# First cross-attention of a decoder: two pairs of score banks, sums turned token-major, three buffers of keys and values

## What is computed

```python
q = x @ Wq.T + bq
k = context @ Wk.T + bk
v = context @ Wv.T + bv
q = q.reshape(B, NQ, 16, 16); k = k.reshape(B, NKV, 16, 16); v = v.reshape(B, NKV, 16, 16)
attn = jnp.einsum('bihd,bjhd->bhij', q, k) * SCALE
attn = jax.nn.softmax(attn, axis=-1)
out = jnp.einsum('bhij,bjhd->bihd', attn, v).reshape(B, NQ, 256)
x = _layernorm(x + out @ Wo.T + bo)
```

## Time and profile before

| | |
|---|---|
| median of 3 runs | 2735.5 us (2731.75 to 2739.67) |
| profiled execution | 2742.5 us, its span 2740.6 us |
| mean granted TensorE clock | 0.86 |
| busy, share of the span | PE 79%, weight loads 55%, DVE 59%, ACT 27%, POOL 33% |
| chain that ended last | PE 58%, DVE 23%, POOL 7%, DMA 4%, ACT 4% |
| of it, `enc_w<-v_all_scratch` DMA | 3% |
| scores L884, PE, x512 | 144.8 us busy; idle before it 120.3 us |
| row maxima L1039, DVE, x128 | 120.3 us busy, 940 ns each |
| shifted scores L897, PE, x1536 | 134.9 us busy |
| exp L1007, ACT, x128 | 93.5 us busy, 730 ns each |
| DMA | 101.22 MB, mean 37 GB/s |

### The profile page before, as it was taken

How to read it: one execution, slowest core, us unless ns; L and a number is a source line. 1 busy time by engine, 2 the same in 40 slices (tenths; PEclk the granted TensorE clock), 3 DMA queues, 4 the chain that set the end, 5 groups by cost and what they waited for, 6 DMA issues and landing times.

```text
span 2740.6 us, 36682 instructions
## 1 busy us (share of the span) xinstructions
PE 2173.6 (79%) x14852; PEld 1517.0 (55%) x14852; DVE 1608.5 (59%) x3034; ACT 734.0 (27%) x1387; POOL 894.8 (33%) x715
## 2 busy tenths in 40 slices
PE   7787777577669997899999999987666786767776
PEld 2333345455546665787888888776454553434532
DVE  7888835355542332455555565566399996455245
ACT  6545232223221122222222222222222221111122
POOL 7886349916300002343534434332200002110000
PEclk9888878788778998899999999998767657888987
DMA  4212233111110001000100100100331010400000
GB/s 135 80 47 85 76 61 105 35 52 46 41 38 30 1 1 73 1 1 1 60 1 1 60 1 1 45 1 1 90 68 34 26 30 24 95 0 0 1 0 27
DMA packets 63592, 101.22 MB, mean 37 GB/s; under 512 B 32361, under 2 KB 56930, under 8 KB 62210
## 3 DMA queue, kind: packets, MB, share of 16 engines
q1 hardware_dynamic: 63426, 98.90, 12.5%
HBM read 78.39 MB, written 20.50 MB: 36 GB/s over the span
## 4 chain that ended last, share of the span: by engine, by line
PE 58%; DVE 23%; POOL 7%; DMA 4%; ACT 4%; issue 3%; SPq 0%; POOLq 0%; DVEq 0%; ACTq 0%
PE PS L1422 8%; PE PS L1438 7%; PE PS L1178 4%; DVE st_h L682 4%; DVE top L2176 3%; PE PS L1157 3%; DVE w_s L2185 3%; PE PS L1339 3%; DMA enc_w<-v_all_scratch 3%; PE PS L884 2%; PE PS L2062 2%; DVE ln_st L265 2%; PE PS L2052 2%; PE PS L1367 2%; DVE XD L1039 2%
## 5 line engine op out<-in xcount | busy, mean ns | idle before, releaser
L284 POOL TENSOR_SCALAR ln_ve<-ln_mv 128x2 f32<-128x2 f32 (+1 forms) x91 | 20.2, 222 | 1491.4 <-DVE ln_mv L268 1491.2
L884 PE MATMUL PS<-enc_w,q_s 32*112 32x375 f32 x512 | 144.8, 604 | 120.3 <-DVE XD L1039 64.3
L1614 DVE TENSOR_TENSOR p_x<-PS,cols 128x1024 f32<-128x1024 f32 x112 | 129.3, 1217 | 147.6 <-PE PS L1384 147.6
L1676 POOL TENSOR_TENSOR q_x<-q_f,cols 128x2048 f32<-128x2048 f32 x56 | 208.7, 3746 | 9.7 <-ACT q_f L1534 9.7
L1039 DVE TENSOR_REDUCE XD<-PS 112x2 f32<-112x750 f32 x128 | 120.3, 940 | 140.0 <-PE PS L884 140.0
L682 DVE TENSOR_TENSOR_SCAN st_h<-dA,st_h 128x3584 f32<-128x3584 f32 x16 | 183.8, 11512 | 0.0
L1007 ACT ACTIVATE e_t<-PS 125x672 f32<-125x672 f32 x128 | 93.5, 730 | 287.0 <-PE PS L897 287.0
L774 POOL TENSOR_TENSOR st_h<-b_s,XD 128x896 f32<-128x896 f32 x56 | 166.3, 3005 | 8.1 <-PE PS L492 6.8
L884 PEld LDWEIGHTS PS<-enc_w,q_s 32*112 32x112 f32 x512 | 51.9, 200 | 162.7 <-DVE XD L1039 97.3
L1242 DVE SCALAR_TENSOR_TENSOR XA<-PS,gate_w,XA 112x256 f32<-112x256 f32 x128 | 61.9, 484 | 135.4 <-PE PS L1178 135.4
L1946 PE MATMUL PS<-dg,e_p 112*125 112x112 f32 x384 | 83.9, 415 | 66.1 <-ACT dg L2130 66.1
(11 more groups left out here) (351 smaller groups left out, 4905.5 us busy)
## 6 DMA issues: line engine op xcount, KB each, us to landing
v_all_scratch<-v_st SPq DMA_DIRECT2D x16, 750.0 KB
enc_w<-v_all_scratch SPq DMA_DIRECT2D x16, 750.0 KB
t_ring<-k_scratch SPq DMA_DIRECT2D x8, 784.0 KB, 12.2
enc_w<-in_enc_w SPq DMA_DIRECT2D x2, 3072.0 KB, 10.6
wc<-in_enc_w SPq DMA_DIRECT2D x2, 3072.0 KB, 10.7
k_all_scratch<-k_st SPq DMA_DIRECT2D x16, 375.0 KB
enc_w<-k_all_scratch SPq DMA_DIRECT2D x64, 93.8 KB
ctx_k<-in_ctx SPq DMA_DIRECT2D x16, 281.2 KB
```

The source lines that it names most:

```text
L884: ins = pe.matmul(ps[a][0:T, 0:S2], q_s[h, m, b * T:(b + 1) * T], k_s[h, b % 2, m, :], start=True, stop=True)
L1614: last = dve.tensor_tensor(p_x[:, m, :, :, :], ps[1][:, m * P:(m + 1) * P].rearrange("p (h i) -> p h i", i=16).unsqueeze(2) .to_broadcast( ...
L1676: last = pool.tensor_tensor(q_x[:, c, :, :].rearrange("p t (h i) -> p t h i", i=16), q_f[:, k % 2, c, :].rearrange("p (t i) -> p t i", i=1 ...
```

## The change

1. Scores have two pairs of banks (0, 1 and 2, 3, by the parity of the pair), and AHEAD is 6; a pair's scores wait for the maximum of the pair before the last. Shifted scores have banks 4 and 5, the weighing bank 6, and all other uses share bank 7, each waiting for the one before it. `nm_w` has four buffers. `slot_uses` gives each use a slot of its own, and a pair of maxima is turned one slot earlier.
2. The sums of a batch are turned to have tokens on partitions (`turn_sums`, 4 matmuls of 112 x 4), inverted there (112 x 16) and spread by 16 matmuls of 32 x 112; DVE multiplies out of PSUM.
3. Keys and values have three buffers; keys and values each have semaphores of their own; values are awaited by `weigh`. Three batches of keys, then the output weights, then three of values and the experts' weights are loaded ahead. `v_t` has moved out of `enc_w0`, `wo4` into it.
4. POOL makes no unit ahead of the first root, then 5, 5 and 4.
5. Each transposed half of the residual has its own signal (`xt_ready`), so later stages count on from `TURNED_X`.

```diff
@@ xat_load @@
-            for b in range(B):
-                if b >= 2:
-                    sp.wait_ge(st_ready, 8 * (b - 1))
...
+            for b in range(3):
+                load_keys(b)
+            sp.dma_start(wo4[:, :, :], dr["wo4"]).then_inc(wo_loaded, 16)
+            sp.wait_ge(y_copied, len(UNITS))
+            for b in range(3):
+                load_values(b)
+            moe_load(sp)
+            for b in range(3, B):
+                sp.wait_ge(st_ready, 8 * (b - 2))
+                load_keys(b)
+                sp.wait_ge(av_done, 4 * (b - 2))
+                load_values(b)
@@ slot_uses @@
-            if at % 2 and 0 <= n + 1 < PAIRS:
-                uses.append(("max", (n + 1) // 2))
...
+            if at % 2 and 0 <= n + 3 < PAIRS:
+                uses.append(("max", (n + 3) // 2))
+            if at == 0 and 0 <= b < B - QB:
+                uses.append(("q", 4 * (b // QB + 1) + b % QB))
...
+            if at == 2 and 1 <= b <= B:
+                uses.append(("rs", b - 1))
+            if at == 4 and 1 <= b <= B:
                 uses.append(("sum", b - 1))
+            if at == 6 and 1 <= b <= B:
                 uses.append(("wo", b - 1))
+            if at in (2, 4) and b > QB and b % QB == 2:
+                uses.append(("xt", 2 * (b // QB) - 2 + (at == 4)))
@@ xat_claim @@
-            if n >= 3:
-                before, j = XAT_USES[n - 3]
+            if n >= 4:
+                before, j = XAT_USES[n - 1]
@@ xat_pe: score @@
-                    if n >= 1:
-                        pe.wait_ge(max_done, n)
+                    if n >= 2:
+                        pe.wait_ge(max_done, n - 1)
                 h = slice(32 * r, 32 * r + 32)
-                ins = pe.matmul(ps[a][0:T, 0:S2], q_s[h, m, b * T:(b + 1) * T], k_s[h, b % 2, m, :],
+                ins = pe.matmul(ps[2 * (n % 2) + a][0:T, 0:S2], q_s[h, m, b * T:(b + 1) * T], k_s[h, b % 3, m, :],
@@ xat_pe: weigh @@
+                if m == 0:
+                    pe.wait_ge(v_loaded[b % 3], V_0[b % 3] + 16 * (b // 3 + 1))
@@ xat_pe @@
+            def turn_sums(b):
+                bank = xat_claim(pe, "rs", b)
+                pe.wait_ge(ot_copied, b + 1)
+                for m in range(4):
+                    last = pe.matmul(bank[0:T, 4 * m:4 * m + 4], o_t[:, m * T:(m + 1) * T], ident[:, 16:P:32],
+                                     start=True, stop=True)
+                last.then_inc(rs_ready, 1)
+
             def spread_sums(b):
                 bank = xat_claim(pe, "sum", b)
-                pe.wait_ge(ot_copied, b + 1)
-                for r in range(4):
-                    last = pe.matmul(bank[32 * r:32 * r + 32, 0:4 * T],
-                                     ident[:, 32 * r + 16:32 * r + 17].to_broadcast([P, 32]), o_t[:, :],
-                                     start=True, stop=True)
+                pe.wait_ge(rs_done, RS_0 + b + 1)
+                for m in range(4):
+                    for r in range(4):
+                        last = pe.matmul(bank[32 * r:32 * r + 32, m * T:(m + 1) * T],
+                                         rs_s[:, 4 * m + r:4 * m + r + 1].to_broadcast([T, 32]),
+                                         ident[0:T, 0:T], start=True, stop=True)
@@ xat_dve @@
-                        link(dve.reciprocal(o_n[:, :], xat_bank("sum", i)[:, 0:4 * T]))
-                        dve.tensor_tensor(o_n[:, :], o_t[:, :], o_n[:, :], ALU.mult).then_inc(divided, 1)
+                        dve.tensor_tensor(o_n[:, :], o_t[:, :], xat_bank("sum", i)[:, 0:4 * T], ALU.mult)\
+                            .then_inc(divided, 1)
@@ xat_pool @@
-                for unit in range(4 * q, min(4 * q + 4, KC * KHIGH)):
+                for unit in range((0, 0, 5, 10)[q], (0, 5, 10, KC * KHIGH)[q]):
```

More of the change, by code:

```diff
@@ L786, in build @@
             sem("kg_arg"), sem("kg_trig"), sem("kg_done"), sem("k_stored"))
-        PAIRS, AHEAD = B * 8, 5
-        kv_loaded, KV_0 = [z_ready, z_abs], len(UNITS)
+        PAIRS, AHEAD = B * 8, 6
+        k_loaded, K_0 = [z_ready, z_abs, bc_ready], (len(UNITS), len(UNITS), NQ)
+        v_loaded, V_0 = [bc_copied, bc_split, u_done], (NQ, NQ, len(UNITS))
+        rs_ready, rs_done, RS_0 = dA_ready, scan_done, 2 * len(UNITS)
         q_ready, q_copied = sem("q_ready"), sem("q_copied")
@@ L841, in build @@
         XAT_AT = {u: i for i, u in enumerate(XAT_USES)}
-        XAT_FREED = {"q": (q_copied, 0), "max": (max_added, 0),
+        XAT_FREED = {"q": (q_copied, 0), "max": (max_added, 0), "rs": (rs_done, RS_0),
                      "sum": (divided, 0), "wo": (wo_added, 0), "xt": (xf_ready, 8), "x1": (xf_ready, 6)}
         def xat_bank(kind, i):
-            return ps[5 + XAT_AT[(kind, i)] % 3]
+            return ps[4 + i] if kind == "q" and i < 4 else ps[7]
         def xat_claim(pe, kind, i):
@@ L909, in weigh @@
                 pe.wait_ge(exp_done, 2 * g + 2)
-                if m == 0 and b >= 1:
-                    pe.wait_ge(ot_copied, b)
+                if m == 0:
+                    pe.wait_ge(v_loaded[b % 3], V_0[b % 3] + 16 * (b // 3 + 1))
+                    if b >= 1:
+                        pe.wait_ge(ot_copied, b)
                 for j in range(JC):
@@ L914, in weigh @@
                         h = 4 * m + r
-                        last = pe.matmul(ps[4][32 * r:32 * r + 32, m * T:(m + 1) * T],
-                                         v_t[0:JR, b % 2, j, 32 * h:32 * h + 32],
+                        last = pe.matmul(ps[6][32 * r:32 * r + 32, m * T:(m + 1) * T],
+                                         v_t[0:JR, b % 3, j, 32 * h:32 * h + 32],
                                          e_t[0:JR, (2 * g + r // 2) % 4, r % 2, j * T:(j + 1) * T],
@@ L943, in turn_input @@
                                         XA[0:T, B - QB + k, i * P:(i + 1) * P], ident[0:T, 0:T])
-                if i == KC - 1:
-                    last.then_inc(xt_ready, 1)
+                last.then_inc(xt_ready, 1)
             def turn_residual(i):
@@ L953, in turn_residual @@
                                         XA[0:T, q * QB + k, c * P:(c + 1) * P], ident[0:T, 0:T])
-                if c == KC - 1:
-                    last.then_inc(xt_ready, 1)
-            shared = {"q": queries, "max": turn_max, "sum": spread_sums, "wo": project,
+                last.then_inc(xt_ready, 1)
+            shared = {"q": queries, "max": turn_max, "sum": spread_sums, "rs": turn_sums, "wo": project,
                       "xt": turn_residual, "x1": turn_input}
@@ L962, in xat_pe @@
                 ahead, uses = n + AHEAD, slot_uses(n)
-                if uses and uses[0][0] == "max":
-                    turn_max(uses[0][1])
                 if 0 <= ahead < PAIRS:
@@ L981, in xat_pe @@
                 for kind, i in uses:
-                    if kind in ("sum", "wo", "xt"):
+                    if kind not in ("q", "x1"):
                         shared[kind](i)
@@ L1006, in xat_act @@
                         act.wait_ge(av_done, n // 2 - 1)
-                    act.activation(e_t[0:JR, n % 4, :, :], PS[0:JR, 2:4, 0:JC * T], ACT.Exp).then_inc(exp_done, 1)
+                    act.activation(e_t[0:JR, n % 4, :, :], PS[0:JR, 4:6, 0:JC * T], ACT.Exp).then_inc(exp_done, 1)
                 for kind, i in uses:
@@ L1049, in xat_dve @@
                 ahead, uses = n + AHEAD, slot_uses(n)
-                if uses and uses[0][0] == "max":
-                    add_max(uses[0][1])
                 if 0 <= ahead < PAIRS:
@@ L1054, in xat_dve @@
                 for kind, i in uses:
-                    if kind == "sum":
+                    if kind == "max":
+                        add_max(i)
+                    elif kind == "rs":
+                        dve.wait_ge(rs_ready, RS_0 + i + 1)
+                        dve.reciprocal(rs_s[:, :], xat_bank("rs", i)[0:T, 0:16]).then_inc(rs_done, 1)
+                    elif kind == "sum":
                         dve.wait_ge(sum_ready, i + 1)
```

73 lines of the change are left out of this document (32 added, 41 removed).

## The result

| | before | changed |
|---|---|---|
| median | 2736.07 us (4 runs, 2731.75 to 2739.67) | 2857.78 us (4 runs, 2853.08 to 2865.01) |
| ratio | 1 | 1.0446, interval 1.0429 to 1.0464 |
| profiled execution, its span | 2742.5, 2740.6 us | 2862.3, 2860.5 us |
| first exp to last exp | 411.7 us | 540.7 us |

The change makes the kernel 4.5% slower. I had forecast 2720 us, in a range of 2655 to 2762: wrong in sign and outside the range.

The account below looks back on a forecast made before the run. Bounds: the score-maximum ring, DMA waits with low clock behind, POOL's stall. Stage 342 + 57 = 399 us against 411.7, with the tail called -15, gave a 2720 us median; own range 2700 to 2745, 8 in 10 2655 to 2762.

Parts of the forecast that it names:

- The ring of 2.02 us: In the kernel before, scores, row maximum and back to PE with one score pair, setting each slot's length.
- Part (a): Stage's slots: two score pairs cut the maximum's wait, even AHEAD queues passes in strips; slot 2.69 us, 342 in all.
- exp ring: Shifted scores, exp and back to shifted scores: 1.82 us, the next limit once two score pairs are used.
- Part (b): Stage's other PE work (projection, spreading, turned sums, queries, residual transposes, norm stalls), paid beyond some 0.4 us free: 57 us.
- rival 2: Stage slower: clock still falls once a batch, 16 stretches costing 42 to 51 us, giving say 2766 us; chance 0.13.
- my own case: The forecast's main case for the whole kernel: granted clock 1.00 through the stage, 2700 to 2745 us, chance 0.58.
- Part (c): Key and value loads: three buffers remove the 51.6 us of waits and each batch's low clock; added early loads cost nothing.
- Part (d): Sums of each batch: 2.96 us of DVE reciprocal go, a 112x16 one comes; DVE is no bound.
- Part (e): First norm: with no POOL unit ahead of the first root, the 16 us stall goes; later groups fit between norms.
- Part (f): Stage's ends: no gain at the start, bounds 0 and 5 us; the tail changes by -1.5 us.
- Rival 1: Strips do not hold each other up: slot 1.82 + 0.06, 103 us less, 2617 us; chance 0.13 (half-way form 2668, 0.10).
- Rival 3: Matmuls on PE start in program order, so second-head scores wait: 32 us slower, 2752 us; chance 0.06.

## Why the prediction was wrong

**Right: what bounds the kernel before, and the mechanism of the strips.** The ring of 2.02 us, the DMA waits, and that with an even AHEAD the passes of a slot queue in their strips. The last was shown from both sides (AHEAD 5 and 7 in the changed kernel, 4 in the kernel before).

**Part (a), the slot: right in kind, too large.** 2.69 us was forecast, 2.44 is measured at the full clock. I had added 2 x 0.40 and 0.06 to the exp ring. In the rows above the second head's score passes start 0.41 us apart and the shifted pass 0.31 behind the second, 0.72 together; and the 0.1 us by which a second strip starts late is not added to them but falls inside, for the score pass starts with the first head's shifted pass. 0.62 is paid and not 0.87. I had also given every slot this length. In a slot with a weighting the exp is done before PE comes to the shifted scores, and PE's own list sets the time. At the full clock:

```profile
588.35 1.77 PE L879 MATMUL PS<-XF,wb 128*128 128x448 f32 x4
590.05 0.78 PE L929 MATMUL PS<-e_t,v_t 125*32 125x112 f32 x24
590.77 0.89 PE L896 MATMUL PS<-enc_w,q_s 32*112 32x375 f32 x4
591.49 0.81 PE L909 MATMUL PS<-q_s,enc_w 32*125 32x112 f32 x12
592.23 0.32 PE L917 MATMUL PS<-ident,XD 112*128 112x112 f32 x1
...
595.38 0.95 PE L939 MATMUL PS<-ident,XD 128*112 128x4 f32 x8
```

Weighting, scores and shifted scores are 2.18 us (590.05 to 592.23).

**Part (b): too small.** I had let 0.4 us of each addition go free. In the slots with a weighting almost nothing is free: the queries are paid with 1.70 (588.35 to 590.05; forecast 1.1). The kernel with both heads' scores first has the same order in these slots, so its exps give the others, as what a slot has above 2.18:

```profile
585.40 0.73 ACT L1024 ACTIVATE e_t<-PS 125x672 f32<-125x672 f32 x1 [1.09 <-PE PS L909]
588.35 0.73 ACT L1024 ACTIVATE e_t<-PS 125x672 f32<-125x672 f32 x1 [2.22 <-PE PS L909]
590.17 0.73 ACT L1024 ACTIVATE e_t<-PS 125x672 f32<-125x672 f32 x1 [1.09 <-PE PS L909]
594.26 0.73 ACT L1024 ACTIVATE e_t<-PS 125x672 f32<-125x672 f32 x1 [3.36 <-PE PS L909]
```

Spreading is paid with 0.77 (585.40 to 588.35; forecast 0.3), the projection with 1.91 (590.17 to 594.26; forecast 1.55). The turned sums, 8 passes in 0.95 (L939 above), are paid with some 0.9 (forecast 0.4).

**The sum of the stage: near at the full clock, by luck.** 60 plain slots of 2.44, 3 of 1.82 at the end and 64 slots of 2.18 are 291 us, where I had 342. Queries (20), turned sums, spreading and projection of 15 batches (53) and some 21 for the three norms and the residual transposes are 94 us, where I had 57. Together that is some 385 us, an estimate from the rows above and the same slots of the scores-first kernel. The forecast of 399 is near it because one term was some 50 us too large and the other some 40 too small.

**The step that failed: rival 2, its price and with it its chance.** By that estimate the lower clock costs some 155 us (540.7 - 385). I had let the clock fall once a batch, for the 6.8 us or so for which it falls behind a DMA wait before, and priced 16 such stretches at 42 to 51 us with a chance of 0.13; my own case had the clock at 1.00 throughout. In fact the clock does not wait for idle time: it is at 0.52 from 422 to 442 us with PE busy in all 20.00, and low for 72% of the stage. My argument against was the end of the stage, a stretch of some 6 us in which shifted scores and weighting alone run at the short times. So short a stretch, with side-by-side slots in front of it, says nothing of 540 us. The trace even has the clock fall right behind it: the next weighting takes 1.35 us in place of 0.78, after 0.82 us of idle time.

```profile
798.07 1.35 PE L915 MATMUL PS<-e_t,enc_w 125*32 125x112 f32 x24 [0.82 <-ACT e_t L1007]
```

The row that did bear on it I had in hand and named: leading pairs of scores on two strips, at the low clock, 1.59 in place of 0.89. It does not settle the matter, since PE is idle 1.04 us ahead of such a pair. But I used it for 6.8 us a batch, when the changed kernel puts two strips at a time into every slot of the stage. The price for a microsecond fits. By it (2.6 to 3.2 us in each 6.8) the 389 us at the lower level cost 149 to 183 us, and 2720 becomes 2869 to 2903. The number of stretches was wrong: these are the length of 57 and not of 16, and the sign was to turn at five.

**Also in rival 2, the link to the layout.** How busy PE is does not tell the kernels apart: it is busy for 98% of the stage with the change (clock 0.64), 96% with AHEAD 5 (0.87), and 81% where scores wait for the maximum again (0.93). The same matmuls, in the same number, had 0.64 one behind the other and 0.87 side by side on different strips, but also 0.78 one behind the other with both heads' scores first. What exactly the chip looks at was not tried, and stays open.

**Part (c), loads: right.** No DMA stands among the stage's waits. Their worth, which the forecast had as 51.6 us and the low clock behind it, measures 74.

**Part (d), reciprocal: right, but I had put its worth at nothing.** It is worth nothing only as DVE time. On the shared bank it would hold PE up for 46 us of the kernel's time. The forecast has no term for the wait of bank 7's next user on DVE.

**Part (e), POOL: right.** The stall of 15.95 us became 1.55. As a gain it was hidden here by the slower stage.

```profile
550.68 0.38 DVE L269 BATCH_NORM_AGGREGATE ln_mv<-ln_st 112x2 f32<-112x6 f32 x4
...
552.61 1.38 DVE L278 TENSOR_SCALAR XA<-XA,ln_mv,ln_rs 112x256 f32<-112x256 f32 x4 [1.55 <-POOL ln_rs L286]
```

**Part (f), ends.** Start 3.9 us earlier (bounds 0 and 5), tail 5.2 less, where I had 1.5. Since the part behind the stage varies by more than that between kernels that have it alike, the 5.2 says little.

**Rivals 1, 3 and 4.** Rival 1 falls: the passes do hold each other up. Slots near its 1.88 us (1.82 and 1.91) are found only where the order or the parity frees the strips. Rival 3 falls with PE's timeline above: the second head's score pass starts at 586.90, and only one pass of the first head's shifted scores has started by then (586.89). The second pass of that matmul, which stands ahead of the score pass in program order, starts at 587.06 or later. Rival 4, no change, falls with the time.

## What to carry to other kernels

In this kernel passes of 32 rows ran side by side on different strips and one behind the other on the same strip. Before changing a pipeline's distance or a bank's parity, write down for one slot which strips its neighbours on the path use, since an index like `2*(n%2)` can undo the overlap that the old distance gave by chance. When a change takes overlap away from PE, price the stage at both clock levels, by rows at each, even where PE is never idle. And put work that does not depend on a wait ahead of it: here that alone gave back 130 of the 195 us that the even distance had cost.

## What the runs showed that I had not expected

- The granted clock lay at the 1.2 GHz level for 72% of a stage in which PE was busy for 98% (0.64), and rose with useless matmuls added: 0.76 and 0.87, with the time falling from 2857.8 to 2846.3 and 2825.7 us.
- Of two fp32 passes of 375 columns in one strip the second starts 0.41 us behind the first, but a shifted pass behind the second starts after 0.31.
- One long hold of a shared bank by DVE (a reciprocal of 2.96 us and a multiplication, sixteen times) cost 46 us, because the small transposes that feed every second slot queue for the same bank.
